# Graph attention plus expert FFN on one core: start, hand-over and end reordered, and W1 split per batch instead of once

## The chip, the cores and the metric

The kernel runs on one core of a Trainium2 chip, as one program. The metric is device time in microseconds (us). Engines are named as in the profile: PE (matrix multiply), DVE (vector), ACT (scalar), POOL (GpSimd), SP (which issues DMAs). They run side by side, each in its own program order, and wait for one another through counting semaphores.

## The reference, cut to what matters

`x` is (16, 512, 128), `adj` (16, 512, 512). There are 8 experts with W1 of 128 x 256 and W2 of 256 x 128.

```
# half 1, for each batch b
h  = layernorm(x);  Wh = h @ W.T;  si = Wh @ a1;  sj = Wh @ a2
e  = leaky_relu(si[:, None] + sj[None, :], 0.2)
att = softmax(where(adj > 0, e, -9e15))
x  = x + elu(att @ Wh)
# half 2
n  = layernorm(x)
w  = router(mean over tokens of n)      # one expert pair per batch
y  = sum over the top 2 experts: gate * (gelu(n @ W1[e] + b1[e]) @ W2[e] + b2[e])
x  = x + layernorm(y + n) * gamma + beta
```

The router needs the token mean of every batch (its load scaling is a sum over batches), so half 2 can't start before half 1 has ended.

## The kernel before, in words

A batch is a tile of 128 partitions with four groups (t = 0 to 3) of 128 tokens. Everything stays in SBUF between the halves. The program of each engine is written out by hand as a list of steps, and these lists set the order; there is no scheduler.

**Attention half.** Step n of DVE (`step` in the vector block) works on batch n's logits (`logits`, L570) and on batch n+1's masked maxima (`masked_max`, L537), and makes the mask of batch n+2 (`make_mask`, L530). `stats1` (L524) and `stats2` (L597) take the statistics of the two layer norms, and `shift_low` (L556) makes the softmax shift. ACT does the leaky part (L966), the exponentials and the scalings. POOL makes the reciprocal square roots (L399), scales the normed rows of half 2 (`scale_x2`, L416) and issues the loads of `adj`. PE transposes logits (L1207), transposes x (L1166), projects (L1175), spreads the sj row over the partitions (`spread_dst`, L1186) and attends (L1222).

**W1.** In the attention half all eight W1 are loaded once, into `w1_parts`. ACT copies them to a rounded "high" part (`split_w1_hi`, four pieces, L1011), and POOL subtracts to get the "low" part (`split_w1_lo`, four pieces, L422). A product in nearly full precision is then three matmuls: low x high, high x low, high x high.

**Hand-over.** The last batch goes through in tiles of 128 tokens (`last_normalize`, `residual_pos_tile`, `norm2_last_tile` on POOL, L427 and L429, `scale_x2_last`, L603). PE sums the tokens (L1294). Then comes the router, a chain of small instructions on DVE, ACT and PE that ends with the expert numbers in `top_idx`. Between its waits PE runs `stay_warm` matmuls (L1285) whose result nobody reads.

**Expert half.** For batch b, PE runs `hidden_part(b)`, 12 matmuls of 512 columns (L1344 to L1346), and `out_part(b)`, 16 of 128 columns (L1359). Its list is h(0), h(1), o(0), h(2), o(1), h(3), o(2) and so on, with h for `hidden_part` and o for `out_part`. SP copies the two chosen W1, high and low, out of `w1_parts` into `w1_pair` (L322) and loads W2 (L330). ACT runs the four GELUs (`apply_gelu`, L1113), makes the high part of the next x2t (`split_hi`, L1045), scales W2 (L1122) and norms (`norm_z`, L1103). DVE's step n in this half starts with `sum_z(n)` (L816), which waits until o(n) is done. Its whole list is sum_z(n), add_beta(n+2) (L805), stats3(n) (L825), split_x2t_lo(n+3) (L662), aggregate3(n) (L834), add_b2(n+2) (L799), scale_gamma(n-1) (L843), finish(n-1) (L853). The b2 rows are mixed by PE, written to DRAM, and loaded back for all partitions by POOL in two DMAs, batches 0 to 3 and 4 to 15 (L467).

The wait of `hidden_part` before the change is on its W1 copy and its x2t parts:

```
if not first:
    pe.wait_ge(s_w1[par], 32 * h + 32 * par)
pe.wait_ge(s_x2lo, b + 1)
```

Of the kernel before, what the change touches and what calls it, by code (L numbers as in the profile page):

```python
# [28 lines left out]
def gat_moe_kernel(nc, x, adj, gnn_w, gnn_a, w_router, b_router, w1, b1, w2, b2, gamma, beta, out):  # L29
# [15 lines left out]
    with ExitStack() as ctx:  # L45
# [16 lines left out]
        ones = sb("ones", [P, P])  # L62
        minus_half = sb("minus_half", [P, T])
# [67 lines left out]
        w1_parts = sb("w1_parts", [P, E, 2, F], F32R)  # L131
# [84 lines left out]
        s_b2mix = [sem("b2_mix_loaded0"), sem("b2_mix_loaded1")]  # L216
        s_n2e = sem("norm2_end_chain")
        s_pick = [sem("first_w1_copied0"), sem("first_w1_copied1")]
        s_x1b = sem("x1b_ready")
        s_x2e = sem("x2_last_tiles")  # L220
        s_w1raw = sem("w1_raw_loaded")
# [52 lines left out]
        WARM = (0, 4, 4, 8)  # L274
        B2_FIRST = 4
# [13 lines left out]
        def _(sp):  # L289
# [16 lines left out]
            for b in range(4):  # L306
                load_x(b)
            for b in range(4, B):
                sp.wait_ge(s_mask, b - 3)
                load_x(b)  # L310
                if b == 5:
                    sp.dma_start(w1_parts[:, :, 1, :].bitcast(F32), w1.rearrange("e p f -> p e f")).then_inc(s_w1raw, 16)
# [19 lines left out]
            sp.wait_ge(s_w1lo, 4)  # L332
            sp.wait_ge(s_x2t_ps, B)
# [26 lines left out]
        def _(pool):  # L360
# [58 lines left out]
            def split_w1_lo(part):  # L419
                es = slice(part * E // 4, (part + 1) * E // 4)  # L420
                pool.wait_ge(s_w1hi, part + 1)
                nc.gpsimd.tensor_tensor(w1_parts[:, es, 1, :], w1_parts[:, es, 1, :].bitcast(F32),  # L422
                                        w1_parts[:, es, 0, :].bitcast(F32), ALU.subtract).then_inc(s_w1lo, 1)

            def norm2_last_tile(t):
                pool.wait_ge(s_mv2, t + 1)
                nc.gpsimd.tensor_scalar(veps2[:, t:t + 1], mv2[:, t, 1:2], LN_EPS, 1.0, ALU.add, ALU.mult).then_inc(s_n2e, 1)  # L427
                pool.wait_ge(s_n2e, 1 + 2 * t)
                nc.gpsimd.tensor_tensor(rstd2[:, t:t + 1], veps2[:, t:t + 1], minus_half[:, t:t + 1],  # L429
                                        ALU.pow).then_inc(s_n2e, 1)  # L430
# [9 lines left out]
            load_adj(0)  # L440
            load_adj(1)
            norms(0)
# [16 lines left out]
            e = pool.value_load(top_idx[0:1, 1:2], min_val=0, max_val=E - 1)  # L459
            pool.wait_ge(s_w1lo, 4)  # L460
            nc.gpsimd.tensor_copy(w1_pair[0][:, 1], w1_parts[:, e]).then_inc(s_pick[1], 1)
# [4 lines left out]
            for i, part in enumerate((slice(0, B2_FIRST), slice(B2_FIRST, B))):  # L466
                nc.gpsimd.dma_start(b2_mix[:, part, :], b2_spread[part, :].rearrange("(a b) d -> a b d", a=1).to_broadcast(  # L467
                    [P, part.stop - part.start, D])).then_inc(s_b2mix[i], 16)

# [18 lines left out]
            def step2(half, n):  # L488
                if in_range(half, n):
                    norm3(half, n)  # L490

# [15 lines left out]
        def _(dve):  # L507
            nc.vector.memset(ones[:], 1.0).then_inc(s_dconst, 1)
# [91 lines left out]
            def scale_x2_last(t):  # L600
                tile = slice(t * D, (t + 1) * D)
                dve.wait_ge(s_n2e, 2 + 2 * t)
# [44 lines left out]
            stats1(2)  # L647
            for t in range(T):
                masked_max(0, t)
            shift_max(0)  # L650
            make_mask(1)
            shift_row(0)
            stats1(3)
            for n in range(B + 1):
                step(n)

# [765 lines left out]
```

## Time and profile before

| | us |
|---|---|
| three timed runs | 293.95, 295.44, 296.98 (median 295.44) |
| the profiled execution, its own time | 294.31 |
| its span in the profile | 292.5 |
| attention half, hand-over and router, expert half | 0 to 158, 158 to 176, 176 to 290 |
| PE, DVE, ACT, POOL busy | 253.4, 234.6, 222.7, 154.2 |

The span is the time from the first to the last instruction; the execution takes 1.8 us more around it. In a timeline row the columns are start, duration, engine, line, operation, output <- input, count, and in brackets the idle time of that engine just before, with what ended it. Matmul ends are modelled, so the start of one matmul to the start of the next says more than its duration.

### The profile page before, as it was taken

The page shows a single profiled execution, that of the slowest core. Times are in us where ns is not written, and L with a number is a line of the kernel's source. Part 1 is how long each engine was busy: PE and PEld are TensorE (multiplying, and loading weights), DVE is VectorE, ACT ScalarE, POOL GpSimd, SP SyncE. Part 2 cuts the span into 40 slices and gives each one's busy share as a digit, 9 for nine tenths or more (in the row PEclk, how much of TensorE's full clock was granted, in tenths as well). Part 3 has the DMA queues.
Part 4 walks back from the last instruction along what each step waited for, and adds up shares of the span by engine and source line. Part 5 has one row for each costly group of instructions (what it writes and reads, how often), then busy time and mean ns, then how long its engine had stood idle before and what let it go on. Part 6 is the DMA issues. An engine that isn't in the chain of part 4 may idle for free.

```text
span 292.5 us, 6644 instructions
## 1 busy us (share of the span) xinstructions
PE 253.4 (87%) x1844; PEld 227.5 (78%) x1845; DVE 234.6 (80%) x668; ACT 222.7 (76%) x509; POOL 154.2 (53%) x239
## 2 busy tenths in 40 slices
PE   5639998999788989999987599499999999999962
PEld 3639987888778878899976347489999999999952
DVE  4297999999999999999997564607778767788756
ACT  2257898998988899999997449277878878888370
POOL 5242187788988897787548712112234432223544
PEclk9977999999999999999999979989999999999999
DMA  6999366543366236440000014832454445545222
GB/s 101 216 197 200 72 111 108 106 89 73 63 108 106 52 63 109 72 75 1 2 1 2 0 39 133 301 106 84 171 180 162 161 146 177 180 163 171 64 72 74
DMA packets 40670, 31.51 MB, mean 108 GB/s; under 512 B 2400, under 2 KB 36608, under 8 KB 40640
## 3 DMA queue, kind: packets, MB, share of 16 engines
q1 hardware_dynamic: 31936, 21.72, 23.3%
q0 software_dynamic: 8704, 9.45, 20.6%
q8 instruction: 12, 0.20, 0.3%
q14 instruction: 18, 0.15, 0.2%
HBM read 27.48 MB, written 4.20 MB: 108 GB/s over the span
## 4 chain that ended last, share of the span: by engine, by line
PE 38%; ACT 5%; issue 4%; POOL 3%; DVE 3%; SPq 3%; DMA 2%; POOLq 0%; DVEq 0%; ACTq 0%
PE banks L1359 16%; PE banks L1344 4%; PE banks L1346 4%; PE banks L1345 4%; PE banks L1222 4%; DMA w_pair<-w_parts 2%; ACT leaky L966 2%; PE banks L1175 1%; PE banks L1207 1%; POOL rstd L429 1%; PE banks L1199 1%; ACT leaky L1113 1%; ACT h_att L976 1%; SPq L321 1%; SPq L330 1%
## 5 line engine op out<-in xcount | busy, mean ns | idle before, releaser
L1222 PE MATMUL banks<-whx,prob_t 128*128 128x129 f32 x512 | 68.2, 277 | 3.7 <-ACT h_att L976 2.5
L1222 PEld LDWEIGHTS banks<-whx,prob_t 128*128 128x128 f32 x512 | 62.0, 192 | 6.8 <-issue 5.7
L416 POOL TENSOR_SCALAR x_all<-x_all,rstd,nb 128x128 f32<-128x128 f32 x60 | 44.2, 748 | 3.1 <-POOL nb L405 3.1
L1207 PE MATMUL banks<-ident,logit 128*128 128x128 f32 x256 | 37.6, 281 | 4.9 <-DVE logit L570 4.1
L481 POOL TENSOR_SCALAR veps<-mv 128x4 f32<-128x4 f32 x15 | 5.9, 393 | 64.0 <-DVE mv L834 64.0
L1001 ACT ACTIVATE prob_t<-banks 128x512 f32<-128x512 f32 x64 | 38.3, 638 | 0.9 <-PE banks L1207 0.8
L1103 ACT ACTIVATE logit<-logit,nb,rstd 128x128 f32<-128x128 f32 x60 | 24.8, 484 | 17.3 <-POOL nb L486 17.3
L1207 PEld LDWEIGHTS banks<-ident,logit 128*128 128x128 f32 x256 | 30.3, 145 | 6.2 <-DVE logit L570 6.0
L399 POOL TENSOR_TENSOR rstd<-var,minus_half 128x8 f32<-128x8 f32 (+1 forms) x20 | 33.7, 1684 | 0.4
L1344 PE MATMUL banks<-x2t_hi,w_pair 128*128 128x512 f32 x64 | 27.3, 426 | 4.1 <-DMA w_pair<-w_parts 3.9
L1359 PEld LDWEIGHTS banks<-w2s,masked_even 128*128 128x128 f32 x256 | 29.7, 192 | 0.5
L1359 PE MATMUL banks<-w2s,masked_even 128*128 128x128 f32 x256 | 29.9, 275 | 0.0
L816 DVE TENSOR_TENSOR logit<-banks,x_all 128x512 f32<-128x512 f32 x15 | 10.4, 691 | 23.2 <-ACT logit L1103 12.5
L1359 PEld LDWEIGHTS banks<-w2s,leaky 128*128 128x128 f32 x224 | 26.1, 192 | 0.5
L966 ACT ACTIVATE leaky<-masked_even,shift_neg 128x512 f32<-128x512 f32 x32 | 21.2, 719 | 6.7 <-DVE shift_neg L556 6.7
L1359 PE MATMUL banks<-w2s,leaky 128*128 128x128 f32 x224 | 26.1, 275 | 0.0
L1346 PE MATMUL banks<-x2t_hi,w_pair 128*128 128x512 f32 x64 | 25.8, 402 | 0.0
L1113 ACT ACTIVATE masked_even<-banks,b_sel 128x512 f32<-128x512 f32 x32 | 19.7, 677 | 7.8 <-PE banks L1346 7.7
L1345 PE MATMUL banks<-x2t_lo,w_pair 128*128 128x512 f32 x64 | 25.7, 401 | 0.0
L966 ACT ACTIVATE leaky<-masked_odd,shift_neg 128x512 f32<-128x512 f32 x32 | 21.3, 720 | 4.7 <-DVE shift_neg L556 4.7
L570 DVE SCALAR_TENSOR_TENSOR logit<-masked_even,shift_pos,leaky 128x512 f32<-128x512 f32 x32 | 23.3, 747 | 0.2 <-ACT leaky L966 0.2
L570 DVE SCALAR_TENSOR_TENSOR logit<-masked_odd,shift_pos,leaky 128x512 f32<-128x512 f32 x32 | 23.1, 745 | 0.3 <-PE banks L1207 0.2
(149 smaller groups left out, 560.8 us busy)
## 6 DMA issues: line engine op xcount, KB each, us to landing
adj_sb<-in_adj_dram POOLq DMA_DIRECT2D x16, 512.0 KB, 6.9
w_pair<-w_parts SPq DMA_DIRECT2D x30, 256.0 KB, 2.3
x_all<-in_x_dram SPq DMA_DIRECT2D x16, 256.0 KB, 2.8
w2r<-in_L_ffn_W_dram SPq DMA_DIRECT2D x32, 128.0 KB, 2.1
out_dram<-prob_t SPq DMA_DIRECT2D x15, 256.0 KB, 2.3
w_parts<-in_L_ffn_W_dram SPq DMA_DIRECT2D x1, 1024.0 KB, 9.2
b_mix<-b_spread POOLq DMA_DIRECT2D x1, 768.0 KB, 7.5
b_mix<-b_spread POOLq DMA_DIRECT2D x1, 256.0 KB, 4.2
```

The lines of the kernel that those rows point to most:

```text
L399: nc.gpsimd.tensor_tensor(rstd[:, kinds, :], var12[:, kinds, :], minus_half[:].unsqueeze(1).to_broadcast([P, 2, T])[:, kinds, :], ALU.pow) ...
L416: nc.gpsimd.tensor_scalar(x_all[:, b, tile], x1_all[:, b, tile], rstd12[c % 4][:, 1, t:t + 1], nb2[c % 2][:, t:t + 1], ALU.mult, ALU.add). ...
L570: nc.vector.scalar_tensor_tensor(out=logit[:, t, :], in0=masked_dst[b % 2][:, t, :], scalar=shift_pos[b % 2][:, t:t + 1], in1=leaky[:, t, ...
L966: nc.scalar.activation(leaky[:, t, :], masked_dst[b % 2][:, t, :], ACT.Identity, bias=shift_neg[:, t:t + 1], scale=ALPHA).then_inc(s_leaky, 1)
L1001: nc.scalar.activation(prob_t[:, t, :], lt_ps[t % 2], ACT.Exp).then_inc(s_prob, 1)
L1103: nc.scalar.activation(zn[par][:, tile], zs[par][:, tile], ACT.Identity, bias=nb3[par][:, t:t + 1], scale=rstd3[par][:, t:t + 1]).then_inc ...
L1207: last = nc.tensor.transpose(lt_ps[t % 2][:, c * P:(c + 1) * P], logit[:, t, c * P:(c + 1) * P], ident[:])
L1222: last = nc.tensor.matmul(into[:, 0:D + 1], prob_t[:, t, c * P:(c + 1) * P], whx[b % 3][:, c, 2:WHX], start=(c == 0), stop=(c == T - 1))
L1344: nc.tensor.matmul(hid_ps[kc], lo, x2t_hi[par][:], start=True, stop=False)
L1345: nc.tensor.matmul(hid_ps[kc], hi, x2t_lo[par][:], start=False, stop=False)
L1346: nc.tensor.matmul(hid_ps[kc], hi, x2t_hi[par][:], start=False, stop=True).then_inc(s_hid_ps, 1)
L1359: last = nc.tensor.matmul(y_ps[par][:, t * D:(t + 1) * D], hidden[par][:, kc, t * P:(t + 1) * P], w2s[par][:, kc // FC, kc % FC, :], start ...
```

## The change

1. **W1 raw.** `w1_parts` becomes `w1_all`, raw. The four pieces of `split_w1_hi` (ACT) and of `split_w1_lo` (POOL) in the attention half are gone. SP now loads the two raw W1 of a batch from DRAM into `w1_raw`. ACT makes the high part for batch n+2 behind GELU n+1, and DVE makes the low part for batch n+2 in its step n, between aggregate3 and add_b2. `hidden_part(b)` waits for that low part. Batch 0 is copied from `w1_all` by ACT and POOL, its low part is made by DVE inside the router chain, and its four low x high matmuls come behind all the others.
2. **b2 in three parts**, batches 0 to 1, 2 to 4 and 5 to 15; the third is issued by POOL in its step 0 of the expert half, behind norm3(0).
3. **The last GELU** stands ahead of norm_z(13) on ACT.
4. **The start.** x of batches 2 and 3 is loaded only after adj 0 has landed, adj 1 only after norms(0). DVE finishes the shifts of batch 0 before make_mask(1), and its step 0 is written out. PE runs 28 matmuls that nobody reads (`keep_busy`, bf16, 128 x 512, in runs of 8, 5, 2, 5 and 8) in the start, where one f32 `warm_up` stood, and spreads the sj row of batch 0 ahead of transposing x of batch 1.
5. **The hand-over.** scale_x2 of batch 14 moves from POOL to ACT, behind the last normalize. POOL norms the last batch in pairs of tiles, not tile by tile. DVE takes the first inverse sum of batch 15 ahead of residual_neg(14), and ACT takes the last probs ahead of last_normalize(0). `stay_warm` runs (6, 2, 2, 7) times, not (0, 4, 4, 8).

The diff, cut to its core:

```diff
@@ sync
-            for b in range(4):
-                load_x(b)
+            load_x(0)
+            load_x(1)
+            sp.wait_ge(s_adj[0], 16)
+            load_x(2)
+            load_x(3)
...
                 if b >= 2:
-                    sp.wait_ge(s_hid_ps, KC * (b - 1))
+                    sp.wait_ge(s_w1lo, b - 1)
...
-                    sp.dma_start(w1_pair[par][:, k].bitcast(F32), w1_parts[:, e].bitcast(F32)).then_inc(s_w1[par], 16)
+                    sp.dma_start(w1_raw[par][:, k, :], w1[e]).then_inc(s_w1[par], 16)
@@ gpsimd
             load_adj(0)
+            norms(0)
             load_adj(1)
-            norms(0)
             norms(1)
...
-            for n in range(B + 1):
+            for n in range(B):
                 step(n)
-                if 5 <= n < 9:
-                    split_w1_lo(n - 5)
-
-            for t in range(T):
-                norm2_last_tile(t)
+            norms(END + NORM_LAG)
+            for i in range(PAIRS):
+                norm2_last_pair(i)
...
+            pool.wait_ge(s_w1raw, 16)
+            for k in range(TOP_K):
+                e = pool.value_load(top_idx[0:1, k:k + 1], min_val=0, max_val=E - 1)
+                nc.gpsimd.tensor_copy(w1_raw[0][:, k, :], w1_all[:, e]).then_inc(s_pick, 1)
@@ vector
+            def split_w1_lo(half, n):
+                b, h, par = batch_at(half, n)
+                if isinstance(half, int) and b == 0:
+                    dve.wait_ge(s_pick, TOP_K)
+                if past(half, b, 2):
+                    dve.wait_ge(s_hid_ps, KC * (b - 1))
+                dve.wait_ge(s_w1hi, b + TOP_K)
+                nc.vector.tensor_tensor(w1_pair[par][:, :, 1, :], w1_raw[par][:], w1_pair[par][:, :, 0, :].bitcast(F32),
+                                        ALU.subtract).then_inc(s_w1lo, 1)
...
             router_steps["gated"] = rc[0]
+            split_w1_lo(0, 0)
...
             split_x2t_lo(0, 2)
+            split_w1_lo(0, 1)
...
                     aggregate3(half, n)
+                if in_range(half, n + 2):
+                    split_w1_lo(half, n + 2)
@@ scalar
             probs(B - 1, 2)
+            probs(B - 1, 3)
             last_normalize(0)
-            probs(B - 1, 3)
...
             last_normalize(3)
+            scale_x2_before_last()
             copy_x2t(B - 2)
...
             split_hi(0, 2)
+            split_w1_hi(0, 1)
...
                     apply_gelu(half, n + 1)
+                if in_range(half, n + 2):
+                    split_w1_hi(half, n + 2)
...
+            apply_gelu(0, B - 1)
             norm_z(0, END - 1)
-            apply_gelu(0, B - 1)
@@ tensor
             project(0)
+            keep_busy(5)
+            spread_dst(0)
             transpose_x(1)
-            spread_dst(0)
+            keep_busy(2)
...
                 pe.wait_ge(s_x2lo, b + 1)
+                pe.wait_ge(s_w1lo, b + 1)
```

How it moves instructions, first on DVE in its second step of the expert half (step 1), before. `logit<-banks,x_all` is sum_z(1), `x2t_lo` the low part of x2t for batch 4, `x_all<-x_all,b_mix` add_b2(3).

```order
446 L816 TENSOR_TENSOR logit<-banks,x_all 128x512 [waits y_in_psum,x2b_ready]
447 L805 TENSOR_TENSOR x_all<-x_all,beta_less_one 128x512
448 L825 BN_STATS bn<-logit 128x6 [waits z_ready,mean_var3]
449 L825 BN_STATS bn<-logit 128x6 x3
450 L662 TENSOR_TENSOR x2t_lo<-x2t_all,x2t_hi 128x512 [waits x2t_high_part_ready,hidden_in_psum]
451 L834 BN_AGGR mv_1<-bn 128x2 [waits bn3_stats]
452 L834 BN_AGGR mv_1<-bn 128x2 x3
453 L799 TENSOR_TENSOR x_all<-x_all,b_mix 128x512
```

The same step of DVE in the changed kernel:

```order
450 L849 TENSOR_TENSOR logit<-banks,x_all 128x512 [waits y_in_psum,x2b_ready]
451 L838 TENSOR_TENSOR x_all<-x_all,beta_less_one 128x512
452 L858 BN_STATS bn<-logit 128x6 [waits z_ready,mean_var3]
453 L858 BN_STATS bn<-logit 128x6 x3
454 L692 TENSOR_TENSOR x2t_lo<-x2t_all,x2t_hi 128x512 [waits x2t_high_part_ready,hidden_in_psum]
455 L867 BN_AGGR mv_1<-bn 128x2 [waits bn3_stats]
456 L867 BN_AGGR mv_1<-bn 128x2 x3
457 L684 TENSOR_TENSOR w_pair<-w_raw,w_pair 128x2x256 [waits w1_high_parts_ready,hidden_in_psum]
458 L832 TENSOR_TENSOR x_all<-x_all,b_mix 128x512
```

One instruction came in, the subtraction that makes the low part of W1 for batch 3, in seventh place behind sum_z(1), which waits for o(1).

PE around the end of o(1) and the start of h(3) in the changed kernel (L1440 is `out_part`, L1427 the first line of `hidden_part`):

```order
444 L1440 MATMUL banks<-w2s,leaky 128x128 [waits w2_scaled,hidden_ready]
445 L1440 MATMUL banks<-w2s,leaky 128x128 x15
446 L1427 MATMUL banks<-x2t_hi,w_pair 128x512 [waits hidden_ready,w1_low_parts_ready,x2t_low_part_ready]
447 L1428 MATMUL banks<-x2t_lo,w_pair 128x512
448 L1429 MATMUL banks<-x2t_hi,w_pair 128x512
```

and the same place before:

```order
440 L1359 MATMUL banks<-w2s,leaky 128x128 [waits w2_scaled,hidden_ready]
441 L1359 MATMUL banks<-w2s,leaky 128x128 x15
442 L1344 MATMUL banks<-x2t_hi,w_pair 128x512 [waits hidden_ready,x2t_low_part_ready,w1_loaded1]
443 L1345 MATMUL banks<-x2t_lo,w_pair 128x512
444 L1346 MATMUL banks<-x2t_hi,w_pair 128x512
```

The order on PE stands; the wait for the DMA of W1 became a wait for the low part that DVE makes.

## Rows read from the trace of the kernel before

**Rows 1.** The page, busy tenths of PE and DVE in 40 slices of 7.3 us

```profile
PE   5639998999788989999987599499999999999962
DVE  4297999999999999999997564607778767788756
```

**Rows 2.** Windows, PE only: stretch, us, busy (instructions), granted clock, DMA share, GB/s

```profile
184.94:188.87 3.93, 0.00 (x1) 1.00 0.91 329
188.87:193.48 4.61, 4.61 (x14) 0.63 0.36 119
228.66:234.99 6.33, 6.33 (x46) 1.00 0.48 164
234.99:241.32 6.33, 6.33 (x46) 1.00 0.50 167
```

**Rows 3.** Timeline of the expert half, DVE and PE, 266 to 274 us

```profile
266.80 0.69 DVE L816 TENSOR_TENSOR logit<-banks,x_all 128x512 f32<-128x512 f32 x1 [1.20 <-ACT logit L1103]
...
269.22 3.73 PE L1359 MATMUL banks<-w2s,leaky 128*128 128x128 f32 x32
...
269.68 0.66 DVE L799 TENSOR_TENSOR x_all<-x_all,b_mix 128x512 f32<-128x512 f32 x1
...
272.79 3.74 PE L1359 MATMUL banks<-w2s,masked_even 128*128 128x128 f32 x32
...
273.13 0.69 DVE L816 TENSOR_TENSOR logit<-banks,x_all 128x512 f32<-128x512 f32 x1 [1.37 <-PE banks L1359]
```

**Rows 4.** Line L662 alone: durations in ns min/median/max, first and last start

```profile
L662 DVE TENSOR_TENSOR x2t_lo<-x2t_all,x2t_hi x16: 673/674/693, 168.9 to 268.8; 128x512 fp32r<-128x512 f32 x16
```

**Rows 5.** Timeline of the attention half, DVE and POOL, and line L556 alone

```profile
60.35 0.68 DVE L530 TENSOR_SCALAR mask<-adj_sb 128x2048 bf16<-128x2048 bf16 x1
...
69.10 0.68 DVE L530 TENSOR_SCALAR mask<-adj_sb 128x2048 bf16<-128x2048 bf16 x1
...
70.96 1.28 POOL L422 TENSOR_TENSOR w_parts<-w_parts 128x512 fp32r<-128x512 f32 x1
...
78.84 0.68 DVE L530 TENSOR_SCALAR mask<-adj_sb 128x2048 bf16<-128x2048 bf16 x1
...
L556 DVE SCALAR_TENSOR_TENSOR shift_neg<-whx,row_max x16: 136/148/1124, 19.1 to 151.0; 128x4 f32<-128x4 f32 x16
```

**Rows 6.** Timeline of the start, PE and DVE, 7 to 32 us

```profile
7.27 2.10 PE L1175 MATMUL banks<-wh_weights,xnt 128*128 128x130 f32 x8 [0.36 <-ACT wh_weights L1049]
...
12.31 0.68 DVE L530 TENSOR_SCALAR mask<-adj_sb 128x2048 bf16<-128x2048 bf16 x1
...
20.13 1.42 DVE L570 SCALAR_TENSOR_TENSOR logit<-masked_even,shift_pos,leaky 128x512 f32<-128x512 f32 x2 [0.20 <-ACT leaky L966]
...
28.31 0.69 DVE L537 CUSTOM_DVE_ANT_0 masked_even<-mask,banks 128x512 f32<-128x512 bf16 x1 [1.94 <-PE banks L1186]
...
31.10 1.13 PE L1175 MATMUL banks<-wh_weights,xnt 128*128 128x130 f32 x8
```

**Rows 7.** Timeline of the hand-over, POOL and DVE, 160 to 167 us

```profile
160.93 1.76 POOL L416 TENSOR_SCALAR x_all<-x_all,rstd,nb 128x128 f32<-128x128 f32 x4 [0.21 <-POOL nb L405]
...
166.82 0.43 DVE L603 TENSOR_SCALAR x_all<-x_all,mv,rstd 128x128 f32<-128x128 f32 x1 [0.56 <-POOL rstd L429]
```

**Rows 8.** Timeline of the first expert batches, ACT and PE, 176 to 189 us

```profile
176.07 2.08 ACT L1113 ACTIVATE masked_even<-banks,b_sel 128x512 f32<-128x512 f32 x3
...
178.47 0.40 PE L1344 MATMUL banks<-x2t_hi,w_pair 128*128 128x512 f32 x1
...
179.25 0.61 ACT L1045 CAST x2t_hi<-x2t_all 128x512 fp32r<-128x512 f32 x1
...
188.87 0.51 PE L1344 MATMUL banks<-x2t_hi,w_pair 128*128 128x512 f32 x1 [3.93 <-DMA w_pair<-w_parts]
```

**Rows 9.** Timeline of the end, ACT, 279 to 283 us

```profile
279.05 1.65 ACT L1103 ACTIVATE logit<-logit,nb,rstd 128x128 f32<-128x128 f32 x4 [3.55 <-POOL nb L486]
...
280.60 2.39 ACT L1113 ACTIVATE leaky<-banks,b_sel 128x512 f32<-128x512 f32 x4
```

More of the change, by code:

```diff
@@ L490, in step2 @@
                     norm3(half, n)
+                if isinstance(half, int) and n == 0:
+                    load_b2(2)
             pipeline(pool, step2, 0, B - 2, 4, 3)
@@ L650, in _ @@
             shift_max(0)
+            shift_row(0)
+            shift_low(0)
+            shift_high(0)
             make_mask(1)
-            shift_row(0)
+            stats1(2)
             stats1(3)
-            for n in range(B + 1):
-                step(n)
+            stats1(4)
+            masked_max(1, 0)
+            logits(0, 0)
+            logits(0, 1)
+            masked_max(1, 1)
+            logits(0, 2)
+            masked_max(1, 2)
+            logits(0, 3)
+            masked_max(1, 3)
+            shift_max(1)
+            make_mask(2)
+            shift_row(1)
+            for n in range(1, B):
+                step(n)
+            def split_w1_lo(half, n):
[7 more added lines that the diff above has]
+                                        ALU.subtract).then_inc(s_w1lo, 1)
             def split_x2t_lo(half, n):
@@ L694, in _ @@
             invert_tile(0)
+            residual_neg(END)
+            stats2(END)
             invert_tile(1)
@@ L1006, in copy_x2t, with scale_x2_before_last @@
                 nc.scalar.activation(x2t_all[:, b, :], tr_ps, ACT.Copy, accum_out=x2_sum[:, b:b + 1]).then_inc(s_x2t, 1)
-            def split_w1_hi(part):
-                es = slice(part * E // 4, (part + 1) * E // 4)
-                act.wait_ge(s_w1raw, 16)
-                nc.scalar.copy(w1_parts[:, es, 0, :], w1_parts[:, es, 1, :].bitcast(F32)).then_inc(s_w1hi, 1)
+            def scale_x2_before_last():
+                b, c = END, END + NORM_LAG
+                act.wait_ge(s_x1, b + 1)
+                act.wait_ge(s_n2, 2 * b + 2)
+                for t in range(T):
+                    tile = slice(t * D, (t + 1) * D)
+                    nc.scalar.activation(x_all[:, b, tile], x1_all[:, b, tile], ACT.Identity, bias=nb2[c % 2][:, t:t + 1],
+                                         scale=rstd12[c % 4][:, 1, t:t + 1]).then_inc(s_x2f, 1)
             def step(n):
@@ L1114, in apply_gelu, with split_w1_hi @@
                                          bias=b1_sel[:, c, bass.ds(b * TOP_K + k, 1)]).then_inc(s_hid, 1)
+            def split_w1_hi(half, n):
+                b, h, par = batch_at(half, n)
+                act.wait_ge(s_w1[par], 32 * h + 32 * par)
+                if not isinstance(half, int) or b >= 2:
+                    act.wait_ge(s_hid_ps, KC * (b - 1))
+                nc.scalar.copy(w1_pair[par][:, :, 0, :], w1_raw[par][:]).then_inc(s_w1hi, 1)
             def scale_w2(half, n):
@@ L1149, in _, with keep_busy @@
         def _(pe):
-            def warm_up(times):
+            def keep_busy(times):
                 for _ in range(times):
-                    nc.tensor.matmul(lt_ps[0], ones[:], whx[0][:].rearrange("p t n -> p (t n)")[:, 0:N],
-                                     start=True, stop=True)
+                    nc.tensor.matmul(lt_ps[0], idle_in[:, 0:P], idle_in[:], start=True, stop=True)
             def transpose_x(b):
@@ L1262, in _ @@
             project(0)
+            keep_busy(5)
+            spread_dst(0)
             transpose_x(1)
-            spread_dst(0)
+            keep_busy(2)
             project(1)
+            keep_busy(5)
             spread_dst(1)
-            for n in range(B - 1):
+            transpose_x(2)
+            keep_busy(8)
+            transpose_logits(0, 0)
+            transpose_logits(0, 1)
+            project(2)
+            transpose_logits(0, 2)
+            attend(0, 0)
+            transpose_logits(0, 3)
+            attend(0, 1)
+            spread_dst(2)
+            attend(0, 2)
+            for n in range(1, B - 1):
                 step(n)
@@ L1347, in hidden_part @@
                                      stop=True).then_inc(s_hid_ps, 1)
-                    if between[kc] is not None:
-                        between[kc]()
             def out_part(half, n):
```

107 lines of the change are left out of this document (58 added, 49 removed).

## The prediction, made before the changed kernel ran

> **What bounds the kernel now.** I read the page's slices first, then the chain of waits, then the timeline around each place that the chain names. The slices show three stages [rows 1]. In slices 5 to 21 of the attention half DVE stands at 9 and PE dips to 7: DVE is the bound. In slices 22 to 27 both have holes (PE 5 and 4, DVE down to 0): the hand-over, the router, and a stall behind it. From slice 28 to 38 PE is at 9 and DVE at 6 to 8: PE is the bound. The windows say the same more sharply [rows 2]. Two neighbouring batches of the expert half take 6.33 us each, in which PE is busy for all 6.33 at full clock, while between 184.94 and 188.87 PE has nothing to do at all. So in the attention half a DVE instruction less is time won, and in the expert half the one thing not to do is to make PE wait between two batches.
>
> **The wait that the change adds.** This is the large term. PE's list is h(0), h(1), o(0), h(2), o(1), h(3): `hidden_part(n+2)` stands directly behind `out_part(n)`. In the changed kernel it waits for the low part of W1 for batch n+2. DVE makes that in its step n, and step n begins with sum_z(n), which waits for o(n). The split is thus queued behind an instruction that can't start until PE has finished the very matmuls in front of the waiting one. However much slack DVE has, PE must stand idle from the end of o(n) until DVE has gone through seventh place of its list. The two order listings above show both ends of this loop. The split of x2t doesn't suffer from it, since it is made one batch earlier (n+3).
>
> Its size, step by step. Where DVE waited for PE alone, sum_z started at 273.13, the next o at 272.79, so 0.34 us after the end of the one before [rows 3]. From sum_z at 266.80 to add_b2 at 269.68, that is over sum_z, add_beta, stats3, split_x2t_lo and aggregate3, it is 2.88 us [rows 3]. In this place the new subtraction is put. The trace has none of it, but L662 is the same operation on as many elements with an output of the same type: 0.67 us, from 0.673 to 0.693 [rows 4]. With 0.06 us for the signal to PE (DVE x_all to PE in such places costs about that; I allow 0 to 0.15), PE waits 0.34 + 2.88 + 0.67 + 0.06 = 3.95 us. Could something cover it? o(n+1) can't, it stands behind h(n+2). The bounds of one wait are 3.8 and 4.3 us, the latter if DVE is late with step n-1, for which there is no reason, as the period becomes 10.3 us.
>
> This wait comes before h(2) to h(14). h(15) is free of it: in front of it stand both o(13) and o(14), and o(14) takes 3.57 us (269.22 to 272.79) [rows 3], while DVE's step 13 has no x2t to split and is through after about 3.4. The wait before h(2) takes the place of the one for a DMA that is there now, 3.93 us [rows 2, 8]. So 12 waits are new: 12 x 3.95 = 47.4 us.
>
> **The clock behind each wait.** The one wait of this length that the trace has was followed by a stretch at lower clock: h(2), 12 matmuls of 512 columns, took 4.61 us from 188.87 on at a mean granted clock of 0.63, part of it at the lower level of 1.2 GHz [rows 2]. At full clock h(n) takes 6.33 - 3.57 = 2.76 us, so this wait cost 1.85 us more. Each of the 12 new ones has the same form. They may cost 0 (if short waits in a row leave the clock alone) to 1.85 each. The low stretch needn't begin when PE starts again, as it did here; where it begins while PE still waits, part of it is free. I take 1.2, two thirds: 12 x 1.2 = 14 us, with bounds 0 and 22.
>
> The Trainium skill, "TensorE: Matmul & The Clock Gate", section "HAM oscillation — how this bites in real kernels", describes such a loop of short work and a wait, in which every round starts cold. By that rule each of the 12 waits pays in full, which is the upper bound above (22 us); this trace agrees as far as one wait shows.
>
> **ACT in the expert half** gets one copy of 0.61 us per batch (as L1045) [rows 8]. With a period of 10.3 us it has room, and I cost it at nothing; without the PE waits it would nearly fill the 6.33 us. SP loads half the bytes for W1, early enough, since the load now waits for the split two batches back.
>
> **The first two batches.** Now GELU of batch 0 starts at 176.07 and h(1) at 178.47 [rows 8]. After the change four things come ahead. ACT copies W1 in two pieces, each with its own register load (about +0.8 us, an estimate from one copy now). DVE puts a split (0.67) into the router chain. The four low x high matmuls come last, so no GELU starts before all else of h(0): about 179.25. And h(1) needs the low part for batch 1, which stands behind four GELUs (2.39, [rows 9]) and two ACT copies (0.61 each), a DVE split of x2t and its own (0.67 each): 179.25 + 2.4 + 1.2 + 1.35 = 184.2, less some overlap 183.8. That is 5.3 us later than 178.47. PE idles nearly 4 us before it, so the clock costs another 1.7; h(1) and o(0) take 6.36, and the wait of 3.95 brings h(2) to 195.8, against 188.87: +6.9 us, with bounds 4 and 9. b2 in three parts helps the DMA traffic in this stretch (DMA share 0.91 in the wait [rows 2]), but the DMA is no longer what comes last; no gain.
>
> **The attention half.** One L556 took 1.12 us against a median of 0.148 [rows 5], and it ends with POOL's split of W1 (70.96 + 1.28 = 72.24). Mask to mask it is 8.75 us without a split and 9.74 with one [rows 5]. There are four: -3.9 us, bounds -3 and -4. This is on the path, since DVE is the bound there.
>
> **The start.** Before, the mask of batch 0 stood at 12.31, behind x 1 and behind two adj and four x sharing the DMA engines; its logits began at 20.13, and DVE waited 1.94 us at 28.31 for PE [rows 6]. PE was slow: eight pieces of L1175 took 2.10 us at 7.27 and 1.13 at 31.10 [rows 6]. The change lets adj 0 land by about 8.5, spreads batch 0 by 9.7 (if PE is fast by then, which keep_busy is made for), ends its maxima by 12.3, but then DVE waits for norms(2) on POOL before stats1(4), to about 16. Logits begin near 18, and batch 2's maxima, at 28.31 now, near 24: -4.3 us. Bounds: -1 (PE stays slow, and the five bf16 matmuls come in the way) and -6.
>
> **The hand-over.** POOL's four scalings (1.76 us at 160.93) go to ACT, the four per-tile chains on POOL, whose last released DVE at 166.82, become two, and the last exponential of batch 15 comes up [rows 7]. ACT gets through its tiles about 1.6 us sooner, POOL's last chain ends about 2.4 sooner. I take -2.4, bounds 0 and -3.5; the ACT scaling in front of copy_x2t(14) is what is late next.
>
> **The end.** Now the last GELU waits for norm_z(13), 279.05 to 280.60 [rows 9]. Put ahead it could run with the matmuls, 3 us earlier, but DVE then waits for norm_z(13) itself. I take -1.3, bounds 0 and -3.
>
> **Sum**, against the profiled execution's own 294.3 us: 294.3 + 47.4 + 14 + 6.9 - 3.9 - 4.3 - 2.4 - 1.3 = 350.7, so 351 us, or 19% more. Its own time is 1.1 us below the median of the runs shown, 295.44; I leave that to the range.
>
> **Rivals.**
> *The waits come, the clock stays up.* Then 14 us and the 1.7 go: 335. For it: DVE signals at regular distances, and PE works 6.3 us of each 10.3. Against it: the row at 188.87. Chance 0.12.
> *Every wait pays in full.* 22 instead of 14: 359. For it: the same row. Chance 0.13.
> *Faster: the split is in time.* If h(n+2) found its low part ready, the place that decides would be ACT's and DVE's fill of the 6.33 us, and all the small gains would stand. The price: 294.3 - 3.9 - 4.3 - 2.4 - 1.3 = 282.4; h(2) would come at about 190.5 instead of 188.87 and without the slow stretch of 1.85, so 282 us. It decides if DVE's split ends before o(n) does, i.e. if sum_z(n) weren't what it is queued behind. I find no way for that in the lists; it stands for a misreading of mine. Chance 0.04.
> *The waits overlap with something I call serial*, say half of the 3.95, and the time ends between 300 and 331: chance 0.05.
> The forecast, 336 to 357, has what is left: 0.66.
>
> Faster by over 1% (about what a measurement of this kernel can tell from no change) 0.04, within 1% 0.01, slower 0.95. The range: the clock staying up gives 335, and the start and the hand-over at their best bounds take 1.7 and 1.1 more, so 332, and 331 with a little of the end; every wait at full price gives 359, and the start at 1 instead of 4.3 would add 3.3, so 362. I give 331 to 362.
>
> **What would show it.** In the changed profile PE's share falls below 80%, its row in the second half shows no 9s in a row, and the costliest idle group is L1427 released by DVE w_pair L684, 13 or 14 times, near 4 us each. Windows of one batch there are 11 to 12 us long with a granted clock near 0.8. POOL's L422 is gone and no L556 is longer than 0.2 us. Batch 2's first maximum starts near 24 us. The forecast is wrong if L1427 follows o(n) within 0.5 us, or if its wait is released by anything other than the low part.

## The result, and the profile after

The changed kernel takes 368.57 us (median of 4 runs, 367.93 to 369.41). The kernel before takes 295.73 beside it (4 runs, 293.95 to 296.98), a ratio of 1.247, with a 95% interval of 1.240 to 1.254. Slower was right, and so was the place. The size was not: 351 was forecast, with 362 as the upper end.

From the page of the changed kernel, the slices of 9.15 us (busy tenths of PE, then the granted clock) and the costliest group:

```profile
PE   7789999999999998976855785578568557755991
...
PEclk9989999999999999969868888986788887689896
...
L1427 PE MATMUL banks<-x2t_hi,w_pair 128*128 128x512 f32 x60 | 35.0, 584 | 55.9 <-DVE w_pair L684 44.4 <-DVE x2t_lo L692 11.4
```

PE's second half has no row of 9s any more like that of [rows 1], only two slices of 9 at its end, and its clock moves between 0.6 and 0.9. L1427 starts `hidden_part`, L684 is the new subtraction. The 11.4 us are the first three of the same waits, put down to another signal.

One batch of the changed kernel, DVE and PE (columns as in [rows 3]):

```profile
258.33 0.69 DVE L849 TENSOR_TENSOR logit<-banks,x_all 128x512 f32<-128x512 f32 x1 [7.84 <-ACT logit L1146]
258.94 0.68 DVE L838 TENSOR_TENSOR x_all<-x_all,beta_less_one 128x512 f32 x1
259.54 0.86 DVE L858 BATCH_NORM_STATS2 bn<-logit 128x6 f32<-128x128 f32 x4
260.32 0.67 DVE L692 TENSOR_TENSOR x2t_lo<-x2t_all,x2t_hi 128x512 fp32r<-128x512 f32 x1
260.91 0.37 DVE L867 BATCH_NORM_AGGREGATE mv<-bn 128x2 f32<-128x6 f32 x4
261.20 0.66 DVE L684 TENSOR_TENSOR w_pair<-w_raw,w_pair 128x512 fp32r<-128x512 f32 x1
...
262.11 0.79 PE L1427 MATMUL banks<-x2t_hi,w_pair 128*128 128x512 f32 x1 [4.12 <-DVE w_pair L684]
```

DVE was idle for 7.84 us ahead of sum_z (L849), then did everything in its list, and the subtraction came last, 2.87 us after sum_z began, just the distance taken from [rows 3]. PE stood for 4.12 us. DVE isn't busy here, it is late by its order.

Windows of the changed kernel, PE, columns as in [rows 2]: four batches from the start of an h to the end of the o behind it, and the `hidden_part` of one of them, h(7), alone:

```profile
187.21:196.54 9.33, 9.33 (x44) 0.68 0.32 105
200.35:208.34 7.99, 7.98 (x44) 0.81 0.24 68
248.62:257.99 9.37, 9.36 (x44) 0.68 0.21 56
275.60:283.50 7.90, 7.90 (x44) 0.82 0.24 66
248.62:253.91 5.29, 5.29 (x13) 0.50 0.30 77
```

The same stretch at full clock, from the run below with the waits filled:

```profile
208.77:215.34 6.57, 6.57 (x44) 1.00 0.26 80
```

(The 6.33 us of [rows 2] run from one h to the next, and a next h that needn't wait starts 0.24 us ahead of the modelled end of o.) So a batch pays either 1.3 to 1.6 us, or 2.8 to 2.9, in which case all of h, and the beginning of o, run at 1.2 GHz. Of the twelve batches h(2) to h(13), seven paid 1.3 to 1.6 and five paid 2.8 to 2.9, together 24.4 us.

Where the clock fell, ahead of h(7), ahead of h(9), and in h(4), which had waited for just as long:

```profile
247.62:248.12 0.50, 0.00 (x0) 0.67 0.00 0
248.12:248.62 0.50, 0.00 (x0) 0.50 0.00 0
274.60:275.10 0.50, 0.00 (x0) 1.00 0.00 0
275.10:275.60 0.50, 0.01 (x1) 0.50 0.00 0
212.15:213.20 1.05, 1.05 (x5) 1.00 0.00 0
213.20:214.30 1.10, 1.10 (x5) 0.71 0.00 0
```

Worked out from such windows (an estimate, to about 0.1 us), the clock fell 0.8 us before h(7) began, 0.5 us before h(9) began, and 1.5 us after h(4) had begun. In all five batches that paid 2.8 to 2.9 it fell 0.7 to 0.9 us before h. In the others up to h(14) it fell 0.3 to 0.5 us before h (h(3), h(5), h(9), h(13)) or 1.1 to 1.5 us after its start (h(4), h(6), h(10), h(14)).

### The profile page after: what moved, and what is told of

Same layout as the page of the kernel before. It is cut to its first block and busy times, and to the rows that moved or that the text cites. A ratio compares the mean times of both kernels' runs of the same rounds, so it can differ in the third digit from the quotient of the medians.

```text
span 366.0 us, 6793 instructions
## 1 busy us (share of the span) xinstructions
PE 285.5 (78%) x1872; PEld 247.3 (68%) x1872; DVE 240.7 (66%) x685; ACT 234.3 (64%) x525; POOL 149.3 (41%) x229
## 3 DMA queue, kind: packets, MB, share of 16 engines
q0 software_dynamic: 8736, 9.45, 17.1%
## 5 line engine op out<-in xcount | busy, mean ns | idle before, releaser
L1427 PE MATMUL banks<-x2t_hi,w_pair 128*128 128x512 f32 x60 | 35.0, 584 | 55.9 <-DVE w_pair L684 44.4
L849 DVE TENSOR_TENSOR logit<-banks,x_all 128x512 f32<-128x512 f32 x15 | 10.4, 691 | 97.5 <-ACT logit L1146 76.1
L484 POOL TENSOR_SCALAR veps<-mv 128x4 f32<-128x4 f32 x15 | 7.0, 470 | 141.8 <-DVE mv L867 139.4
L1427 PEld LDWEIGHTS banks<-x2t_hi,w_pair 128*128 128x128 f32 x60 | 16.7, 278 | 62.3 <-issue 42.5
L1156 ACT ACTIVATE masked_even<-banks,b_sel 128x512 f32<-128x512 f32 x32 | 21.6, 687 | 49.1 <-PE banks L1429 46.5
L1156 ACT ACTIVATE leaky<-banks,b_sel 128x512 f32<-128x512 f32 x32 | 21.7, 687 | 45.2 <-PE banks L1429 45.0
L420 POOL TENSOR_SCALAR x_all<-x_all,rstd,nb 128x128 f32<-128x128 f32 x56 | 42.3, 766 | 2.9 <-POOL nb L409 2.9
L1429 PE MATMUL banks<-x2t_hi,w_pair 128*128 128x512 f32 x60 | 33.3, 554 | 0.0
L1428 PE MATMUL banks<-x2t_lo,w_pair 128*128 128x512 f32 x60 | 33.0, 550 | 0.0
L1440 PEld LDWEIGHTS banks<-w2s,masked_even 128*128 128x128 f32 x256 | 30.8, 197 | 0.8
L1440 PE MATMUL banks<-w2s,masked_even 128*128 128x128 f32 x256 | 30.5, 279 | 0.0
L1440 PEld LDWEIGHTS banks<-w2s,leaky 128*128 128x128 f32 x224 | 29.2, 208 | 1.3
L1440 PE MATMUL banks<-w2s,leaky 128*128 128x128 f32 x224 | 28.2, 287 | 0.0
```

The source lines that it names most:

```text
L420: nc.gpsimd.tensor_scalar(x_all[:, b, tile], x1_all[:, b, tile], rstd12[c % 4][:, 1, t:t + 1], nb2[c % 2][:, t:t + 1], ALU.mult, ALU.add). ...
L1156: nc.scalar.activation(hidden[par][:, kc, :], hid_ps[kc], ACT.Gelu, bias=b1_sel[:, c, bass.ds(b * TOP_K + k, 1)]).then_inc(s_hid, 1)
L1427: nc.tensor.matmul(hid_ps[kc], lo, x2t_hi[par][:], start=True, stop=False)
L1428: nc.tensor.matmul(hid_ps[kc], hi, x2t_lo[par][:], start=False, stop=False)
L1429: nc.tensor.matmul(hid_ps[kc], hi, x2t_hi[par][:], start=False, stop=True).then_inc(s_hid_ps, 1)
L1440: last = nc.tensor.matmul(y_ps[par][:, t * D:(t + 1) * D], hidden[par][:, kc, t * P:(t + 1) * P], w2s[par][:, kc // FC, kc % FC, :], start ...
```

## The experiments

Eleven kernels were run. The first four start from the changed kernel and ask how much of the loss is the place of the subtraction, how much is the wait, and how much the clock.

**The split ahead of sum_z.** One step of DVE's list is moved:

```diff
+                if in_range(half, n + 2):
+                    split_w1_lo(half, n + 2)
                 if in_range(half, n):
                     sum_z(half, n)
...
                     aggregate3(half, n)
-                if in_range(half, n + 2):
-                    split_w1_lo(half, n + 2)
```

> The changed kernel with one call moved on DVE: the W1 low part of batch n+2 is made ahead of sum_z(n), no longer behind aggregate3(n). Theory L (the loop): PE waited before h(n+2) only because the split was queued behind sum_z(n), which waits for o(n). Then all waits on L684 from h(2) on go, a batch takes 6.33 us again, and the clock stays at full: of 151.5 us between h(2) and h(14) 75.5 go, with h(1) and h(14) some 5 more, so 287 us. Rival S (no slack): ACT's copy and DVE's split don't fit beside the other work of a 6.33 us batch, and a batch takes 6.6 to 7.0 us: 291 to 296 us. Rival D (the data come late, from DRAM, whatever the order): above 330 us.

It took 289.17 us (287.39 to 290.74), 0.979 of the kernel before, interval 0.973 to 0.985. The end of one batch, in this kernel's timeline:

```profile
204.39 0.67 DVE L692 TENSOR_TENSOR x2t_lo<-x2t_all,x2t_hi 128x512 fp32r<-128x512 f32 x1
...
207.28 0.68 DVE L684 TENSOR_TENSOR w_pair<-w_raw,w_pair 128x512 fp32r<-128x512 f32 x1
...
208.29 0.48 PE L1427 MATMUL banks<-x2t_hi,w_pair 128*128 128x512 f32 x1
```

The same subtraction now ends at 207.96, 0.3 us before h(6) starts, and PE doesn't wait. So 79 us hung on the place of one instruction of 0.67 us. That is work moved, not removed, and there is hardly any slack. For the next batch the rows are:

```profile
213.91 0.69 DVE L684 TENSOR_TENSOR w_pair<-w_raw,w_pair 128x512 fp32r<-128x512 f32 x1
...
214.84 0.49 PE L1427 MATMUL banks<-x2t_hi,w_pair 128*128 128x512 f32 x1
```

h(7) starts 0.24 us behind the end of the subtraction (in the changed kernel, where PE stood waiting for it, that was 0.25), and 6.55 us behind h(6), not 6.33. Before it, ACT's copy waited 0.33 us for the DMA of the raw W1. h(9), h(11) and h(13) are late by 0.2 us in the same way, some 0.9 us in all. That much of rival S is there; the rest is theory L.

**The wait filled.** In the changed kernel PE runs 14 matmuls nobody reads ahead of each h from batch 2 on.

```diff
                 if in_range(half, n + 1):
+                    if past(half, n + 1, 2):
+                        for _ in range(14):
+                            nc.tensor.matmul(banks[:, 6, :], mask[:, 0, 0:P], mask[:, 1, :], start=True, stop=True)
                     hidden_part(half, n + 1)
```

> The changed kernel with 14 matmuls that nobody reads (bf16, 512 columns, into a free PSUM bank, 3.0 us at full clock) ahead of each hidden_part from batch 2 on. Theory C (the clock is a term of its own): the waits on L684 end when they did, 3.8 to 4.1 us behind the end of o(n), but PE is busy in them, the granted clock stays near 1.0, and a batch takes 6.33 + 4.0 = 10.3 us instead of 12.6. 13 times 2.3 us less: 338 us. Rival: the 2.3 us per batch beyond the wait come from something else (memory traffic of the raw W1, say): 365 us or more.

It took 343.7 us (one run). From its timeline:

```profile
211.61 3.73 PE L1440 MATMUL banks<-w2s,leaky 128*128 128x128 f32 x32
215.40 2.97 PE L1471 MATMUL banks<-mask 128*128 128x512 bf16 x13
219.29 0.49 PE L1427 MATMUL banks<-x2t_hi,w_pair 128*128 128x512 f32 x1 [0.93 <-DVE w_pair L684]
```

h still starts only when DVE has split, but every batch now runs at full clock: the periods from h(2) to h(14) are 10.4 to 10.7 us instead of 11.8 to 13.5. The kernel is 25 us faster with more work, and from h(2) to h(15) the two traces take 137.2 and 163.1 us, 25.9 apart. That is theory C in its mechanism, though 338 was expected; the rival asked for 365 or more. So the clock is a cost of its own beside the waits, and it is near 25 us, not 14. The mean period is 10.60 us at full clock, so a wait by itself costs 10.60 - 6.33 = 4.27 us.

**The split in second, and in fourth place.** It goes directly behind sum_z, or behind stats3:

```diff
                     sum_z(half, n)
+                if in_range(half, n + 2):
+                    split_w1_lo(half, n + 2)
```

> The changed kernel with the split directly behind sum_z(n), in second place. Theory L gives a wait of 0.34 + 0.61 + 0.67 + 0.06 = 1.7 us before h(2) to h(14) instead of 3.8 to 4.1. If so short a wait leaves the clock alone, 287 + 13 x 1.7 = 309 us; if every wait is followed by a slow stretch whatever its length, 13 x 1.5 or more on top: 330 us.

> The changed kernel with the split behind sum_z, add_beta and stats3. Theory L gives a wait of 0.34 + 0.61 + 0.60 + 0.78 + 0.67 + 0.06 = 3.1 us. 287 + 13 x 3.1 = 327 us if the clock stays up at that length; 345 to 360 us if each such wait is followed by one slow stretch (1.5 to 1.8 us) or two (about 3 us).

Second place: 321.98 us (one run), waits of 1.6 to 1.9. Between the two expectations, and its timeline shows why. Starts of h with the wait before them, and of the o behind:

```profile
209.70 0.49 PE L1427 MATMUL banks<-x2t_hi,w_pair 128*128 128x512 f32 x1 [1.72 <-DVE w_pair L684]
212.56 3.73 PE L1440 MATMUL banks<-w2s,masked_even 128*128 128x128 f32 x32
...
226.59 0.49 PE L1427 MATMUL banks<-x2t_hi,w_pair 128*128 128x512 f32 x1 [1.81 <-DVE w_pair L684]
231.03 3.73 PE L1440 MATMUL banks<-w2s,masked_even 128*128 128x128 f32 x32
236.65 0.49 PE L1427 MATMUL banks<-x2t_hi,w_pair 128*128 128x512 f32 x1 [1.89 <-DVE w_pair L684]
241.12 3.74 PE L1440 MATMUL banks<-w2s,leaky 128*128 128x128 f32 x32
```

From h to o it is 2.86 us in the first pair, 4.44 and 4.47 in the others, with nearly the same wait ahead. Of the 13 batches h(2) to h(14), five in a row, h(7) to h(11), paid 1.3 to 1.6 us and eight nothing. Fourth place: 353.59 us (one run), waits of 2.9 to 3.3, periods of 9.5 to 12.6. It lies in the upper of the two expectations: eleven of the 13 waits of this length pay, those before h(3) and h(5) don't. The changed kernel, with waits of 3.8 to 4.1, pays always.

The next kernel starts from the first of these runs, to see whether more is to be had. All but one of those behind it start from that one and price single edits; the one on POOL's subtraction starts from the kernel before.

**The first pair of batches.** In the run with the split ahead, h(1) still waited 3.24 us, behind four GELUs. Both its split steps move up:

```diff
@@ scalar
+            split_w1_hi(0, 1)
             apply_gelu(0, 0)
             split_hi(0, 2)
-            split_w1_hi(0, 1)
@@ vector
+            split_w1_lo(0, 1)
             dve.wait_ge(s_gb, 32)
...
             split_x2t_lo(0, 2)
-            split_w1_lo(0, 1)
```

> The run with the split ahead of sum_z, and besides for batch 1 alone: ACT makes the high part of W1 ahead of the first four GELUs and DVE the low part ahead of the first add_beta. There h(1) started at 174.58 after a wait of 3.24 us and ran at the lower clock (4.9 us instead of 2.8). Theory F: h(1) is held by the place of its split alone, so it starts near 171.2, right behind h(0), and without the wait the slow stretch is gone as well (-2.1): about -3.4 - 1.5 = -5, 284 us. Rival G: what is gained there is given back, since ACT and DVE fill nearly the whole batch later and o(0) waits for its scaled W2: 287 to 289, with new gaps of PE before o(0) or in the later batches. Rival H: the slow stretch comes all the same behind some shorter gap: 286.

It took 282.91 us (6 runs, 281.74 to 283.96), 0.953 of before, interval 0.949 to 0.956. Theory F: h(1) follows h(0) without a wait, and from the expert numbers to h(2) it is 15.4 us instead of 20.5 in the two profiles, 5.1 less. Its window from o(0) into o(14), PE:

```profile
176.07:264.70 88.63, 88.63 (x623) 1.00 0.42 126
```

PE is without a gap and at full clock. The 13 batches from o(0) to o(13) took 83.16 us: nine of 6.33, and four of 6.55, late by the same 0.2 us as above. That is better than the kernel before, whose h(2) waited for a DMA [rows 8].

**POOL's subtraction in the kernel before, made small.** It covers 4 columns of 256, so most of the low parts are left out of the result.

```diff
-                nc.gpsimd.tensor_tensor(w1_parts[:, es, 1, :], ...
+                nc.gpsimd.tensor_tensor(w1_parts[:, es, 1, 0:4], ...
```

> The kernel before, with POOL's four subtractions for the low part of W1 cut to 4 columns of 256 (most of the low parts are left out of the result: they hold the unsplit W1). ACT's four copies for the high parts stay. Theory P (the prediction's term of -3.9): it is POOL's subtraction that holds one small DVE instruction for about 1 us each, so four masks follow 8.75 instead of 9.74 us after the one ahead, no L556 takes over 0.2 us, and the time is 3.9 us lower, 291.4 (ratio 0.987). Rival Q: the longer distance comes from ACT's copies, or there is slack later: 294.5 to 296.

It took 292.02 us (4 runs) beside 296.81, a ratio of 0.982, interval 0.977 to 0.988: 5.2 us less by the ratio, 3.7 to 6.8 by its interval (4.8 between the medians). L556 in this kernel, min, median and max in ns:

```profile
L556 DVE SCALAR_TENSOR_TENSOR shift_neg<-whx,row_max x16: 132/142/157, 19.1 to 146.6; 128x4 f32<-128x4 f32 x16
```

The longest is 157 ns, against 1124 in [rows 5], and the four masks in question follow 8.75 to 8.87 us after the one ahead. ACT's four copies were still there. Theory P. In the kernel before, the long L556 beside the POOL row of [rows 5] is

```profile
71.15 1.12 DVE L556 SCALAR_TENSOR_TENSOR shift_neg<-whx,row_max 128x4 f32<-128x4 f32 x1
```

That a small DVE instruction can be held until a POOL instruction beside it has ended is what the Trainium skill gives in "SBUF — State Buffer", section "SBUF: two separate sides": the port pair they share is a lock, held for the whole instruction, by a DVE operation with two inputs in SBUF or by one of POOL. The trace agrees: L556 ends at 72.27, POOL's subtraction at 72.24, and with a POOL instruction of 0.22 us none is held. No run here shows the lock itself.

**The last GELU behind norm_z(13) again.**

```diff
-            apply_gelu(0, B - 1)
             norm_z(0, END - 1)
+            apply_gelu(0, B - 1)
             norm_z(0, END)
```

> As the run with the first pair of batches mended, but the last GELU stands behind norm_z(13) again. Read from the profile, from the start of h(15) to the end of the span. Theory E (the prediction's term of -1.3): the tail is 1.3 us longer than with the GELU ahead. Rival R (what the changed kernel seems to show, -0.5): 0.3 to 0.7 us longer, since h(15) and last_out_part come ahead only until DVE waits for norm_z(13).

One run, 284.07. From the start of h(15) to the end of the span it is 281.8 - 264.7 = 17.1 us, and in the run with the first pair mended 281.7 - 266.3 = 15.4. So 1.7 us for this edit: theory E, a little more. The two spans are equal nevertheless, since in this run's start PE stayed at full clock where it fell in the other, and its fourth mask followed the third after 7.6 us, not 9.1. The GELU's row with the edit undone, and the one ahead of it:

```profile
267.51 1.65 ACT L1146 ACTIVATE logit<-logit,nb,rstd 128x128 f32<-128x128 f32 x4 [3.56 <-POOL nb L489]
...
269.06 2.38 ACT L1156 ACTIVATE leaky<-banks,b_sel 128x512 f32<-128x512 f32 x4
```

ACT sat idle for 3.56 us, as in [rows 9]. In the run with the GELU ahead it starts 1.04 us behind h(15) (267.33 and 266.29). By that, its input was ready at 265.8 here, 1.7 us before ACT came to norm_z(13), which is the difference measured.

**The start without its 28 unread matmuls, and with eight more.**

```diff
-                for _ in range(times):
+                for _ in range(0):
```

> As the run with the first pair of batches mended, but without any of the 28 keep_busy matmuls in the start. Theory K (what the start's term of -4.3 leaned on): PE then runs the first projections at the lower clock (eight L1228 take 2.1 instead of 1.2 us), the sj row of batch 0 comes a good 1 us later, and the first logits with it: +1 to +2 us. Rival M: the first mask waits for the DMA of x and adj until 9.7 anyway and PE falls to the lower clock again at 20 us in either case, so the matmuls are worth under 0.5 us: same time within 0.5 us.

```diff
             transpose_x(2)
-            keep_busy(8)
+            keep_busy(16)
```

> As the run with the first pair of batches mended, with 16 instead of 8 keep_busy matmuls ahead of the first transposed logits. In that run PE was idle there for 1.96 us and then ran the next 16 matmuls (L1262 and L1228, from 19.71 on) in 3.7 us instead of the 2.1 of full speed. Eight more of 0.236 us fill the gap to 19.65. Theory W (the start's term of -4.3 came out at -2.3 because PE falls to the lower clock a second time in that gap): the next 16 matmuls then take 2.1 to 2.4 us, mask 3 follows mask 2 in 7.6 instead of 9.1 us, and the time falls by 1.0 to 1.6 us: 281.3 to 281.9. Rival V: DVE bounds that place anyway, or the fall comes in a later gap: within 0.5 us of 282.9.

Without them: 285.24 us (6 runs, 284.38 to 286.36), 2.3 more than with them, intervals of the ratios 0.957 to 0.965 against 0.949 to 0.956. Theory K, a little above its +1 to +2. With eight more: 282.17 (6 runs, 282.01 to 282.60), ratio 0.954, interval 0.950 to 0.958. Against the ratio of 0.953 with eight that is no difference that the measurement tells. PE ahead of and in the first logits, with 8 and then with 16:

```profile
15.87 1.89 PE L1210 MATMUL banks<-idle_in 128*128 128x512 bf16 x8
19.71 1.77 PE L1262 MATMUL banks<-ident,logit 128*128 128x128 f32 x8 [1.96 <-DVE logit L576]
21.28 1.94 PE L1228 MATMUL banks<-wh_weights,xnt 128*128 128x130 f32 x8
```

```profile
15.81 3.62 PE L1210 MATMUL banks<-idle_in 128*128 128x512 bf16 x16
19.80 1.32 PE L1262 MATMUL banks<-ident,logit 128*128 128x128 f32 x8 [0.37 <-DVE logit L576]
20.96 1.06 PE L1228 MATMUL banks<-wh_weights,xnt 128*128 128x130 f32 x8
```

The slow stretch is gone in the second profile, as theory W had it, but the gain of 1.0 to 1.6 us that it priced doesn't show. The run with the last GELU moved had the same gap of 1.95 us with 8 matmuls, and ran fast behind it (1.32 and 1.06 as well), so such a gap draws the slow stretch in some executions only. That would fit the narrower spread of the runs with 16 (0.6 us against 2.2), though six runs of each are few.

**x of batch 1 behind adj 0.**

```diff
-            load_x(1)
             sp.wait_ge(s_adj[0], 16)
+            load_x(1)
```

The statistics of x 1 move behind the first maxima.

> As the run with the first pair of batches mended, with x of batch 1 loaded only after adj 0 has landed, and its statistics behind the first maxima. The prediction had adj 0 landed by 8.5; the first mask stood at 10.4 to 10.6, behind x 1 (9.7). Theory X: x 1, adj 0 and x 0 share the DMA engines, so adj 0 alone lands by about 8.3 and the first maximum starts when PE has spread the row, at 9.8 instead of 11.2; the first logits come up to 1.3 us earlier: 281.6 to 282.4. Rival Y: the first logits are paced by the chain x 1, its statistics, POOL's root, statistics of x 4, which now starts later: no gain or +1 us, 283 to 284.

It took 285.21 us (6 runs, 283.20 to 287.23): theory Y, and worse. From its DVE timeline:

```profile
8.73 0.69 DVE L536 TENSOR_SCALAR mask<-adj_sb 128x2048 bf16<-128x2048 bf16 x1 [2.91 <-DMA adj_sb<-in_adj_dram]
...
14.12 0.76 DVE L530 BATCH_NORM_STATS2 bn<-x_all 128x6 f32<-128x256 f32 x2 [1.70 <-DMA x_all<-in_x_dram]
```

adj 0 did land by 8.7, and the first maxima started 1.3 us sooner. But x 1 landed at 14.1 instead of 9.9, for it now shares with adj 1, and the first logits came at 20.8 instead of 18.9.

**b2 in two parts again.**

```diff
-        B2_PARTS = (0, 2, 5, B)
+        B2_PARTS = (0, 4, B)
...
-                if isinstance(half, int) and n == 0:
-                    load_b2(2)
```

> As the run with the first pair of batches mended, with b2 in two parts again (batches 0 to 3, 4 to 15), both loaded ahead of the expert half. Theory N (the prediction put no time on b2 in three parts): same within 0.5 us, 282.9. Rival D: the 768 KB of the second part now collide with the loads of W1 and W2 for batches 2 and 3, as they did in the kernel before (DMA share 0.91 in the wait of 3.93 us ahead of h(2)), and since h(2) now also needs ACT's and DVE's split behind that load, it comes 2 to 4 us later, with a slow stretch behind: 285 to 289.

It took 283.79 us (6 runs, 283.17 to 285.73), ratio 0.961, interval 0.957 to 0.965, against 0.949 to 0.956. So the third part is worth 0.9 us by the medians and about 2.5 by the ratios, between the two theories. add_b2(0) waits 3.0 us for its rows, against 1.6 with three parts. In its trace h(2) starts 7.66 us behind h(1), not 6.81: 0.85 us of PE's time in the place that rival D named, without the slow stretch.

## Why the prediction was right and wrong

Term by term, from the two traces (spans 292.5 and 366.0, 73.5 us apart; the sum had 56.4). The measured column is the distance between the two traces, place by place:

| term | predicted | measured |
|---|---|---|
| 12 new waits of PE | +47.4 | +51.1 |
| slow clock behind them | +14 (0 to 22) | +24.4 |
| first two batches | +6.9 | +6.6 |
| POOL's split of W1 gone | -3.9 | -3.9 |
| start | -4.3 | -2.3 |
| hand-over | -2.4 | -2.1 |
| end | -1.3 | -0.5 |

The measured terms add up to 73.3.

**The waits** were right in place and number, and nearly in size: 3.95 each was forecast, and ten of the twelve are 3.95 to 4.14 in the brackets, two 3.81, 48.2 in all. Reading DVE's own order against the two rows of sum_z and add_b2 gave that within 2%. (The subtraction is the sixth step of that list, not the seventh; the sum has the right five ahead of it.) Two pieces were priced too low. PE began 0.25 us behind the end of the subtraction (261.86 to 262.11), not 0.06. And a bracket starts at the modelled end of o, 0.24 us behind where a next h could have started, which makes 4.26 per batch and 51.1 in all; the run with the waits filled has 4.27. The run with the split ahead took the waits away.

**The step that failed is "The clock behind each wait".** It took one row, the wait for a DMA in [rows 2], as the most that such a wait can cost, and two thirds of it as likely: 1.2 each, 22 us as the bound. The twelve new waits have 1.3 to 1.6 in eight cases and 2.8 to 2.9 in four, 23.2 in all, and h(2) pays 1.2 more than it did before, together 24.4. The run with the waits filled confirms it from the other side, with 25 us. Of the 17.5 us by which the profiled execution (368.24) lies above the 350.7 of the sum, this term has 10.4, the waits 3.7, and the start 2.0.

The row itself was read too high. The 4.61 us in [rows 2] hold 14 matmuls, and h(2) has 12:

```profile
188.87:193.32 4.45, 4.45 (x12) 0.62 0.37 123
```

At full clock h takes 2.84 us up to the start of o (208.29 to 211.13 in the run with the split ahead), so this wait had cost 1.6 and not 1.85. It was one of the cheap kind. The rival "every wait pays in full" had the right mechanism, all thirteen pay, but its price was wrong as well, since it multiplied the same row.

The reason given for less, that part of the slow stretch might fall into the wait, did come true in nine of the thirteen batches h(2) to h(14), by 0.3 to 0.9 us. But the five dearest batches are all among these nine, so it was no sign of a cheap one. The Trainium skill, "TensorE: Matmul & The Clock Gate", section "HAM oscillation — how this bites in real kernels", named in the prediction, has every round of such a loop start cold. The trace agrees for these nine, with a clock of 0.50 when h began. In the other four h began at full clock (1.00 in 212.15 to 213.20), and the measurement decides: they paid all the same, 1.6 each.

**The start** gave -2.3. Two steps of it fell short. "adj 0 lands by about 8.5" was to bring the mask forward with it. The mask stood at 10.40, not 12.31, directly behind the statistics of x 1, for whose load DVE waited to 9.72. The run with x 1 behind adj 0 shows that 8.7 is to be had, and that it doesn't pay. And PE fell back to the lower clock by 19.2 us, in a gap of 2.66 us which the step had not looked for. The rows of the changed kernel that answer to [rows 6]:

```profile
6.71 1.16 PE L1228 MATMUL banks<-wh_weights,xnt 128*128 128x130 f32 x8 [0.40 <-ACT wh_weights L1092]
...
10.40 0.68 DVE L536 TENSOR_SCALAR mask<-adj_sb 128x2048 bf16<-128x2048 bf16 x1
...
18.42 1.41 DVE L576 SCALAR_TENSOR_TENSOR logit<-masked_even,shift_pos,leaky 128x512 f32<-128x512 f32 x2
...
19.23 1.97 PE L1262 MATMUL banks<-ident,logit 128*128 128x128 f32 x8 [2.66 <-DVE logit L576]
...
26.04 0.69 DVE L543 CUSTOM_DVE_ANT_0 masked_even<-mask,banks 128x512 f32<-128x512 bf16 x1 [1.36 <-PE banks L1239]
```

**POOL's split** is the term that came out to the tenth in the trace, and the run with the small subtraction shows the cause. **The hand-over** ended 2.1 sooner (expert numbers at 163.7 against 172.0, less the 6.2 from before it), by the trace alone. **The first two batches** came as forecast, and the run that mends them shows what they cost: 5.1 us between the traces, 6.3 between the medians (289.17 to 282.91), about 7.7 by the ratios (0.979 to 0.953), which are each taken beside their own runs of the kernel before. **The end** gave only 0.5 here, though the edit is worth 1.7 where ACT and DVE are full.

**The rival "faster: the split is in time"** was priced at 282. The order it asks for was not in the changed kernel, but with two small moves it comes to 282.9. The sum fits within about a microsecond, and that is in part luck. From the expert numbers to h(2) the rival had 1.6 us more than the kernel before, and the mended kernel has 1.5 less (15.4 against 16.9), about as much better as the start and the end fell short.

The best version is the changed kernel with `split_w1_lo(n + 2)` ahead of `sum_z(n)` and batch 1's splits brought forward: 282.91 us with 8 unread matmuls ahead of the first logits (ratio 0.953) and 282.17 with 16 (0.954), close to 5% less than the kernel before.

## What to carry to other kernels

Where an instruction is added to an engine, look first at what it stands behind: a 0.67 us subtraction behind an instruction that waits for PE cost 79 us, and hardly anything when placed one step ahead of it. Put what the next stage of the bound engine needs in front of whatever waits for its present stage. A wait of the matmul engine has two prices, its length and the slow stretch behind it; take the second from several rows, and give it a wide upper end when there is only one.

## What the hardware showed beside this

The slow stretch behind a wait of about 4 us isn't of one length. It cost 1.3 to 1.6 us or 2.8 to 2.9, in the same loop, and behind waits of the same length: 3.81 us before h(2), which paid 2.8, and before h(3), which paid 1.4. The dear ones are those where the clock fell 0.7 to 0.9 us before PE began again. What decides when it falls was not found out.

Waits well below that aren't safe either. Waits of 1.8 to 1.9 us, repeated each batch, left the clock alone in some batches and cost 1.3 to 1.6 us in others. One gap of 1.95 us in the start was followed by the lower clock in one profile and not in another.
